# Large attentions: transposing a batch's first head one slot later, and waiting for the queries' low half after a key projection

## What is computed

```
qh = (q_in @ wq + bq).reshape(b, q_len, H, K)
kh = (kv_in @ wk + bk).reshape(b, t, H, K)
logits = jnp.einsum('bqhk,bthk->bhqt', qh, kh) / scale
weights = jax.nn.softmax(logits, axis=-1)
ctx = jnp.einsum('bhqt,bthk->bqhk', weights, vh).reshape(b, q_len, H * K)
return ctx @ wo + bo
```

## Time and profile before

| | |
|---|---|
| three runs | 2279.72, 2285.13, 2288.86 us, median 2285.13 |
| profiled execution, its own time | 2283.49 us |
| its span, first to last instruction | 2281.6 us |
| its mean granted TensorE clock | 0.998 of full |
| TensorE busy | 2222.9 us, 97% of the span |
| VectorE busy | 1376.4 us, 60% |
| ScalarE busy | 1120.4 us, 49% |
| GpSimd busy | 647.0 us, 28% |

### The profile page before, as it was taken

How to read it: one execution, slowest core, us unless ns; L and a number is a source line. 1 busy time by engine, 2 the same in 40 slices (tenths; PEclk the granted TensorE clock), 3 DMA queues, 4 the chain that set the end, 5 groups by cost and what they waited for, 6 DMA issues and landing times.

```text
span 2281.6 us, 36274 instructions
## 1 busy us (share of the span) xinstructions
PE 2222.9 (97%) x12347; PEld 2005.4 (88%) x12347; DVE 1376.4 (60%) x3070; ACT 1120.4 (49%) x2282; POOL 647.0 (28%) x945
## 2 busy tenths in 40 slices
PE   7999999999999999999999999999999999999999
PEld 6777788888999899899888898999899899888888
DVE  6877774524666666666654616666666566554743
ACT  5777753344455454455453434555455455453421
POOL 2111055421232332232322212233233133133421
PEclk9999999999999999999999999999999999999999
DMA  5422136566988888988975557987988988864110
GB/s 190 147 91 104 57 100 201 171 234 193 293 255 280 276 272 258 285 271 260 299 217 151 200 170 239 291 271 243 293 273 254 277 282 262 269 211 137 52 54 33
DMA packets 327767, 480.04 MB, mean 210 GB/s; under 512 B 65822, under 2 KB 250034, under 8 KB 327586
## 3 DMA queue, kind: packets, MB, share of 16 engines
q1 hardware_dynamic: 327586, 477.73, 65.9%
HBM read 368.72 MB, written 108.92 MB: 209 GB/s over the span
## 4 chain that ended last, share of the span: by engine, by line
PE 78%; DMA 8%; DVE 5%; issue 3%; SPq 3%; ACT 2%; POOL 1%; DVEq 0%; ACTq 0%; POOLq 0%
PE ps_o L1880 7%; PE ps_o L1882 7%; PE ps_o L1881 7%; PE ps_v L1880 5%; PE ps_k L1880 5%; PE ps_k L1881 5%; PE ps_k L1882 5%; PE ps_v L1882 5%; PE ps_v L1881 5%; DMA turned_probabilities<-blocks 5%; PE ps_t L1881 4%; PE ps_t L1882 4%; PE ps_t L1880 4%; PE ps_s L1880 4%; PE ps_s L1882 3%; PE ps_s L1881 3%
## 5 line engine op out<-in xcount | busy, mean ns | idle before, releaser
L944 POOL TENSOR_TENSOR pt_lo<-pt_lo,pt_hi 128x512 fp32r<-128x512 f32 x186 | 243.1, 1334 | 201.0 <-ACT pt_hi L1216 201.0
L1251 ACT ACTIVATE prob<-ps_s,row_columns 128x376 f32<-128x376 f32 x256 | 147.1, 575 | 249.9 <-DVE row_columns L1648 248.1
L937 POOL CAST k_hi<-xk_hi 128x1 fp32r<-128x1 f32 x256 | 53.0, 207 | 680.3 <-PE ps_s L1882 680.2
L1666 DVE STREAM_TRANSPOSE blocks<-prob 128x384 f32<-128x384 f32 x240 | 138.8, 579 | 148.0 <-DMA turned_probabilities<-blocks 141.2
L1880 PE MATMUL ps_k<-cs_hi,w_a_hi 128*128 128x376 f32 x636 | 217.8, 342 | 0.0
L1881 PE MATMUL ps_k<-cs_lo,w_a_hi 128*128 128x376 f32 x636 | 213.0, 335 | 0.0
L1882 PE MATMUL ps_k<-cs_hi,w_a_lo 128*128 128x376 f32 x636 | 211.7, 333 | 0.0
L1536 DVE TENSOR_SCALAR prob<-prob,row_columns 128x375 f32<-128x375 f32 (+1 forms) x384 | 204.6, 533 | 4.5
L892 POOL TENSOR_TENSOR w_b_lo<-w_raw_b,w_b_hi 128x512 fp32r<-128x512 f32 x80 | 108.5, 1381 | 332.7 <-ACT w_b_hi L996 332.7
L1648 DVE TENSOR_REDUCE row_columns<-ps_s 128x1 f32<-128x376 f32 x256 | 139.0, 543 | 95.5 <-PE ps_s L1882 95.3
L1880 PE MATMUL ps_t<-cs_hi,w_a_hi 128*128 128x376 f32 x512 | 172.1, 336 | 7.5 <-DVE q L1529 7.5
(11 more groups left out here) (291 smaller groups left out, 6288.7 us busy)
## 6 DMA issues: line engine op xcount, KB each, us to landing
ckd<-context_by_key_halves SPq DMA_DIRECT2D x256, 384.0 KB, 6.2
cs_hi<-context_halves SPq DMA_DIRECT2D x64, 752.0 KB, 7.1
cs_lo<-context_halves SPq DMA_DIRECT2D x64, 752.0 KB, 8.6
pt_lo<-turned_probabilities SPq DMA_DIRECT2D x248, 192.0 KB, 3.7
turned_probabilities<-blocks SPq DMA_DIRECT2D x60, 768.0 KB, 5.4
w_raw_b<-in_blocks_b SPq DMA_DIRECT2D x104, 256.0 KB, 3.8
w_raw_a<-in_blocks_a SPq DMA_DIRECT2D x104, 256.0 KB, 5.2
q<-q_scratch SPq DMA_DIRECT2D x64, 256.0 KB, 5.4
```

What stands on the lines that cost most here:

```text
L937: pool.tensor_copy(k[t % 2][0][:, LK:KW], xk[0][:, ds(col, 1)])
L944: pool.tensor_tensor(lo, lo.bitcast(F32), hi, ALU.subtract).then_inc(t_lo, 1)
L1251: act.activation(prob[buf][:, 0:KW], ps_s[buf][:, 0:KW], ACT.Exp, bias=max_neg[:, buf:buf + 1], accum_out=prob_sum[:, buf:buf + 1]).then_i ...
L1666: dve.transpose(image(place).rearrange("p (s j t e) -> p t j s e", s=4, j=3, t=NT)[:, t], prob[buf][:, 0:BLOCKS * SQUARE].rearrange("p (j ...
```

## The change

There are two edits, and both only reorder. On DVE, the transposes leave `normalized_1` for a function `squares`. For the second to fourth head it is called straight after `normalized_1`, as before. For a batch's first head, which is normalised in slot 2 of the batch before, it is called in slot 3, after that slot's low half of the key (and after the second `output` where there are outputs). On PE, the wait for `q_lo` in slot 2 moves from ahead of the slot's key projection to behind it. No instruction is added or taken away.

```diff
                     normalize(place.unit + t, prob[buf], buf, extra_probability, slice(0, P))
-                    if place.final:
-                        return
+
+                def squares(place, t):
+                    buf = t % 2
                     dve.wait_ge(s_norm, place.unit + t + 1)
                     if t == 0:
                         wait(dve, blocks_out, 16 * (turned_batches(place) - (place.head and place.parity)))
...
                         for head in heads(place, t)[1:2]:
                             output(quad_before(place), head)
+                        if t == 3 and not place.final and not place.next().final:
+                            squares(place.next(), 0)
...
                         if place.key(t + 2):
-                            normalized_1(*place.key(t + 2))
+                            following, head = place.key(t + 2)
+                            normalized_1(following, head)
+                            if head and not following.final:
+                                squares(following, head)
...
-                        if t == 2 and not place.final:
-                            pe.wait_ge(q_lo, place.batch + 2)
                         if place.key(t + 3):
                             key(*place.key(t + 3))
...
                         if t > 1 and query_piece(place, 3):
                             last_piece(place, t)
+                        if t == 2 and not place.final:
+                            pe.wait_ge(q_lo, place.batch + 2)
                         for summed, d in chunks(place, t):
                             context_sum(summed, d)
```

More of the change, by code:

```diff
@@ L1698, in between @@
                             normalized_1(place, 0)
+                            squares(place, 0)
                             key_lo(place, 2)
@@ L1701, in between @@
                             normalized_1(place, 1)
+                            squares(place, 1)
                     last_query(query, a, between, FIRST_PIECES)
```

## The result

The changed kernel takes 2291.08 us (median of 9 runs), the kernel before 2283.78 us (median of 9): ratio 1.0033, 95% interval 1.0021 to 1.0046. It is slower by 7.3 us. That is clear of the noise and inside the 0.5% that I had called no change. The profiled execution took 2293.09 us, the one before 2283.49.

What follows compares the result with a forecast made beforehand. TensorE (PE), busy for 97% of the span, was taken to bound the kernel. The terms summed as 2283.49 - 0.27 - 0 + 5.1 = 2288.3, taken as 2288 us, range 2279 to 2296.

Steps and rivals of the forecast that it cites:

- The ring gives nothing back: Loop outside PE (T3, store, loads, pt_hi, k_hi, k_lo, maximum, exponential): removed 5.5 and 7.5 us return at sums_lo and pt_lo.
- PE's early arrival leaves the ring as it is: Before the outputs: PE arriving 0.57 us sooner waits 2.24 us for sums_lo instead of 1.67; value 0.
- T0's own gain: At 943.91, where the chain goes store, T0, k_lo, PE: moving T0 behind k_lo wins up to 0.27 us.
- The q_lo wait: Eight PE waits for queries, 7.5 us, vanish but return as pt_lo waits before the context sums; value 0.
- T0 ahead of the maximum: In 18 batches T0 (0.58 us) delays slot 3's maximum on DVE; 3.4 us of cover, so cost 0.
- The clock: Joined PE gaps at five places before the outputs: three falls to half clock, 1.7 us each, +5.1 us.
- rival B: Faster: the k_lo and q_lo waits, 13.0 us, stay won, 2270.5 us, or 2260.5 with sums_lo's; chance 0.08.
- D: Slower: T0 in front of the maximum makes PE wait for scores; at the extreme 36 us, 2319; chance 0.05.
- Q: Rival stated with the experiments: the loss sits in PE's moved wait for q_lo; 2291 with that edit alone; no chance given.
- C: Slower by the clock at joined gaps: seven further falls, each 1.7 us exposed, 2295.4 us; chance 0.09.

Runs made afterwards that it cites:

- the repeat: The changed kernel once more, unaltered, timed against the kernel before on another occasion: ratio 1.0046.
- T0 only: Kernel before with only the DVE edit, transposes behind k_lo; the wait for q_lo stays ahead of the key projection: ratio 1.0023.
- q_lo only: Kernel before with only the wait for q_lo moved behind the key projection: ratio 1.0006.

## Why the prediction was right, point by point

- **The ring gives nothing back.** Right in kind. The 5.5 and 7.5 us reappeared at sums_lo and pt_lo, at the place in the earlier trace rows to 0.1 us (2.24 worked out, 2.33 measured). In the total the two rows grew by 18.6 us where 13 were expected, 19.9 and 16.7 for "about 15" each. The longest gap is 3.65 us, not 3.2. The profiled execution waited 5.6 us longer than the step "PE's early arrival leaves the ring as it is" allows. That excess is not steady: the sum of the four rows, 36.6 us here, is 34.8 in the repeat, 31.4 with T0 only and 29.9 with q_lo only, against 31.0 before. What makes it vary is open.
- **T0's own gain, 0.27 us.** Too small to be seen. T0 only is 5.2 us slower, so it is not visible as a gain either.
- **The q_lo wait, 0 us.** Right: 1.0006 with 1 inside the interval, pt_lo up, q gone. Whether it has a part in the loss is not shown. The falls at the first batches are not that part: T0 only has the same ones.
- **T0 ahead of the maximum, 0 us.** Right: with the same order and the outputs' gaps filled, the ratio was 1.0008, that of the kernel before with the same filling 1.0009.
- **The clock, +5.1 us.** The term that carried the forecast, and its sign and size are right. I took three more falls of 1.7 us. The profiled execution has exactly three more behind the outputs (four for one), at a measured 1.54 us: 4.6 us. In the repeat the six stretches behind the outputs took 27.23 to 29.82 us, together 5.9 us more than in the kernel before. What was wrong is that each gap was taken for one fall or none: the repeat has four gaps with a fall, two of them double. Nor does length alone decide. Gaps of 2.28 and 2.33 us had a fall, gaps of 2.35 and 2.72 had none.
- **What no term had.** The profiled pair differs by 9.6 us, and 4.6 of them are these falls. Another 3.4 us lie in the two batches ahead of the six gaps, from the fourth head's exponential in the fourth batch to that in the sixth: 246.1 us before, 249.4 after, 2.1 of it around the wait at 1621.88. The repeat took 246.0 there, so this part came and went with the execution. The rest lies outside these stretches.
- **2288 against 2291.08.** 3 us low, inside the range of 2279 to 2296. The change in time was forecast at 4.8 us and is 7.3, and 10.5 in the second measurement. The mechanism was right; that the first number came so near the forecast is partly luck, as the two measurements differ by 3.2 us between themselves.

What fell: rival B (nothing was won), D (shown by filling), Q. What stands of C: at seven further falls I had 2295.4, 11.9 us more. The 7.3 us are a little over half of that, and the second measurement's 10.5 are near it.

The section on HAM oscillation in the Trainium skill's "TensorE: Matmul & The Clock Gate" says that idle gaps between bursts of matmuls return the array to half rate. The runs agree in kind: gaps before the outputs of 2.3 to 3.7 us brought four falls where gaps of 1.4 to 2.2 us had brought one, and unread matmuls in them took the falls away.

## What to carry to other kernels

Before counting a removed wait as a gain, ask what releases the engine's next wait. If that comes from a chain which the engine does not drive (here a store, its loads and two engines' work), the time is only handed on. Handing it on is not free on TensorE: gaps of 0.57 and 1.67 us kept the clock in the kernel before, and the one of 2.33 us that took their place had 1.5 us lost behind it. Not every longer gap does this, and some shorter ones do (1.48 us in the run with the outputs' gap filled). So shorten the chain that releases the last wait, at just the places where it is late, and count the stretches at half clock before and after every edit.

## What the runs showed of the hardware that had not been expected

- A fall of the clock behind the outputs' gap costs about 1.5 us here. Stretches of the same instructions take 27.23 us without and 28.77 us with one, in two kernels (one of five took 28.70). With a double fall one took 29.82 us in the repeat. At the first batches, where waits follow, taking the falls away brought back 0.8 us and nothing.
- Nine overwritten matmuls (1.9 us) in a gap that PE has anyway kept the clock at 1.00 there. They added no time to five of six stretches (27.23 or 27.24 us) and 0.67 us to one.
- The mean granted clock, read from the timed runs, gives most of the change's cost: 4.6 of 5.2 us, 9.8 of 10.5, 4.8 of 4.8, 4.1 of 5.7 and 2.7 of 3.4 in five comparisons in which only the change or its half differs, and 2.5 for 1.4 with q_lo only. No single one is exact, each ratio being known to some 3 us. Where matmuls were added or pt_hi was moved, it explains little, since those edits cost or gain elsewhere.
- A matmul that already waits for three semaphores put a fourth wait into an instruction of its own (62 of them, with q_lo only too, and none with T0 only). No time could be put on these.
